# Splitting the experts' block-diagonal fp32 matmuls of an early-fusion network into 64x64 blocks on the four quadrants of TensorE, on one Trainium2 core

## The chip, the cores and the metric

The kernel runs on one core of one Trainium2 chip, in one launch. The metric is device time in microseconds (us) of one execution, the median of several runs. TensorE is called PE here (PEld for its weight loads), VectorE is DVE, ScalarE is ACT, GpSimd is POOL and SyncE is SP.

## What is computed

A small fusion network over 4 batches: a token embedding of `x` (a DFT over patches and a linear layer), concatenation with 77 text tokens, and four residual layers, each behind a layer norm, on a hidden state of 4 batches x 1101 tokens x 64 features. The change is in the second layer, a dense mixture of 8 experts. Cut to what matters:

```python
def _L0_ffn_ref(x, Wr, br, W1, b1, g1, be1, m1, v1, W2, b2, g2, be2, m2, v2, Wo, bo):
    feat = jnp.mean(x, axis=0)
    w = jax.nn.softmax(feat @ Wr + br, axis=-1)
    h = jnp.einsum('bfd,edh->bfeh', x, W1) + b1
    h = jax.nn.relu(_bn(h, g1, be1, m1, v1))
    h = jnp.einsum('bfeh,ehk->bfek', h, W2) + b2
    h = jax.nn.relu(_bn(h, g2, be2, m2, v2))
    y = jnp.einsum('bfeh,ehd->bfed', h, Wo) + bo
    return jnp.einsum('bfed,fe->bfd', y, w)
```

The other layers are an mLSTM (before it), a Mamba block with a selective scan, and a token-selecting MLP (both behind it). All data is fp32.

## The kernel before, in words

**Layout.** Features lie on partitions. Two batches share the 128 partitions: batch 2p on partitions 0 to 63 and batch 2p+1 on 64 to 127, for the pairs p = 0 and 1 (`NPAIR` = 2). The hidden state `H` is [128, 2, 1104], tokens on the free axis (1101 padded to 1104). The tokens go in `NG` = 3 groups of `G` = 368. So that one matmul can do both batches of a pair, the host makes each 64x64 expert weight into a 128x128 block-diagonal one (`diag2` in `pack`); half of such a matrix is zero. PSUM is one tensor `PS` of 8 banks.

**The expert stage** walks n = 0 to 23, which is 3 token groups x 8 experts (k = n // 8, e = n % 8), with one instruction stream on each engine, in program order, tied by semaphores:

- PE, per n, in this order: `layer2(n)` (line 584), `layer1(n+1)` (line 575), `spread_weight(n+1)` (line 592), `layer3(n-1)` (line 600). `layer1`, `layer2` and `layer3` are one 128x128 matmul of 368 columns for each pair p, so two each; an fp32 matmul is two instructions, two passes over the data, in the trace. `layer1` writes banks 2 and 3, `layer2` banks 4 and 5, and `layer3` accumulates over the 8 experts in banks 0 and 1. At the eighth expert `layer3` also adds the experts' output bias by a matmul with `ebias` for each pair (line 605). `spread_weight` is one bf16 matmul that spreads the expert's gate weight over all partitions, into bank 6 or 7.
- ACT, in this order: `hidden2(n)` (line 1023), then `hidden1(n+1)` (line 1015). Each is one activation of 128x736 (both pairs) that reads two PSUM banks and applies the batch norm and the ReLU. Both are recorded by the helper `f`, line 882. The helper serves the whole kernel, so rows of line 882 are told apart by their tiles: those of the experts read `PS,bn_shift,bn_scale`.
- DVE: one multiplication by the spread gate weight (line 1463, 128x736), whose result layer 3 reads; after each eighth expert also the residual addition into `H` (line 1468, 128x736).

**The waits.** `layer2(n)` waits for `hidden1(n)` (its data) and for `hidden2(n-1)` (its banks). `hidden2(n)` waits for `layer2(n)`. `layer1(n+1)` waits for `hidden1(n)` (its banks), `spread_weight(n+1)` and `layer3(n-1)` for the DVE's product of n-1. `layer3` at the first expert of a group waits for the residual addition of the group before. The DVE's product of n waits for `hidden2(n)` and the spread weight.

**Around it.** Ahead of the stage stand the router's logits, its softmax and its transposes (lines 557 to 565). Behind it stand the third layer norm (`ln_pe`, lines 293 and 300; the first of its matmuls waits for all three residual additions, line 622) and `in_proj` of the Mamba block (lines 641 and 646), whose matmuls have 64 rows and 128 columns of weights, two at a time, from partitions 0 to 63 and 64 to 127 into different banks. The longest stage is the selective scan. Its `add_y` (line 735) issues fp32 matmuls with 128 rows and 32 columns of weights, whose outputs go to four different strips of 32 partitions of one bank.

Of the kernel before, what the change touches and what calls it, by code (L numbers as in the profile page):

```python
# [10 lines left out]
ALU = mybir.AluOpType  # L11
# [14 lines left out]
NPAIR = B // 2  # L26
# [4 lines left out]
G = SP // NG  # L31
CG = NC // NG
HC = 64 // L
E = 8
# [42 lines left out]
def build(nc, x, txt, wdft, wts, wexp, bn, out, dbg=None):  # L77
    lay, nw = places(WEIGHTS)
    elay, ne = places(EXPERTS)
    with ExitStack() as ctx:  # L80
# [5 lines left out]
        def s(name):  # L86

            if name not in sems:
                sems[name] = ctx.enter_context(nc.semaphore(name))
            return sems[name]  # L90

        PS = ctx.enter_context(nc.psum_tensor("PS", [128, 8, 512], F32))
        W_ = sb("weights", [128, nw])

        def w(name):
            a, n = lay[name]
            return W_[:, a:a + n]
# [6 lines left out]
        H = sb("hidden", [128, NPAIR, SP])  # L104
        pool_ = sb("pair_arrays", [128, 10, NPAIR, SP])
        P1, P2, P3, P4, P5, P6, P7, P8, P9, P10 = (pool_[:, i] for i in range(10))
# [48 lines left out]
        def ew(name, e):  # L155
            a = elay[name][0] + e * 128
            return EW[:, a:a + 128]

        def twin(a, i):

            return a.rearrange("p a t -> p (a t)")[:, i * NPAIR * G:(i + 1) * NPAIR * G].rearrange("p (a t) -> p a t", a=NPAIR)

        h1b, h2b, hwb = P2, P3, P4
# [7 lines left out]
        wT = P5[:, 0, :]  # L171
# [88 lines left out]
        def cols(k):  # L260
            return slice(k * G, (k + 1) * G)

        def half(b):
            return slice(64 * (b % 2), 64 * (b % 2) + 64)
# [141 lines left out]
        def _(pe):  # L406

            pe.wait_ge(s("w_dft_in"), 16)
            for g in range(NOG):
                last = nc.tensor.matmul(PS[:, 4 + g // 4, (g % 4) * OG * PATCH:(g % 4 + 1) * OG * PATCH],  # L410
                                        wd[:, g * 128:(g + 1) * 128], dft, start=True, stop=True)
# [33 lines left out]
            for i in range(NPAIR):  # L445
                last = nc.tensor.transpose(PS[:, 4, i * TXT:(i + 1) * TXT], txt_sb[:, i * 128:(i + 1) * 128],
                                           w("ident")[0:TXT, 0:TXT])
# [20 lines left out]
            for g, (p, k) in enumerate(groups):  # L468
                pe.wait_ge(s("nq_ready"), p + 1)
                if g >= 2:  # L470
                    pe.wait_ge(s("den_ev"), g - 1)
                nc.tensor.matmul(PS[:, 6 + g % 2, 0:G], w("ones"), ik[:, p, cols(k)],
                                 start=True, stop=True).then_inc(s("den_ps"), 1)

            pe.wait_ge(s("gates_ev"), 3 * NGR)
            for n in range(NL):
                lag, p = n // NPAIR, n % NPAIR
# [4 lines left out]
                for k in range(NG):  # L482
                    last = nc.tensor.matmul(PS[:, NG * p + k, 0:size], w("ones"), prod[n % 4][:, k * size:(k + 1) * size],  # L483
                                            start=True, stop=True)
# [35 lines left out]
            for u in range(NPAIR * NT):  # L520
                n = seq_of(u % NT)[1]
# [22 lines left out]
            for g, (p, k) in enumerate(groups):  # L544
                pe.wait_ge(s("msq_in"), p + 1)
                if g >= 2:
                    pe.wait_ge(s("rms_ev"), g - 1)
                nc.tensor.matmul(PS[:, 6 + g % 2, 0:G], w("ones"), WV[1][:, p, cols(k)],
                                 start=True, stop=True).then_inc(s("msq_ps"), 1)
# [19 lines left out]
            pe.wait_ge(s("ln_ln"), 2 * NGR)  # L569
            NX = NG * E  # L570

            def layer1(n):
                if n >= 1:
                    pe.wait_ge(s("h1_ev"), n)
                for p in range(NPAIR):
                    last = nc.tensor.matmul(PS[:, 2 + p, 0:G], ew("E1", n % E), P1[:, p, cols(n // E)],  # L576
                                            start=True, stop=True)
                last.then_inc(s("l1_ps"), 1)

            def layer2(n):  # L580
                pe.wait_ge(s("h1_ev"), n + 1)
                if n >= 1:
                    pe.wait_ge(s("h2_ev"), n)
                for p in range(NPAIR):
                    last = nc.tensor.matmul(PS[:, 4 + p, 0:G], ew("E2", n % E), twin(h1b, n % 2)[:, p, :],  # L585
                                            start=True, stop=True)
                last.then_inc(s("l2_ps"), 1)

            def spread_weight(n):
                if n >= 2:  # L590
# [4 lines left out]
            def layer3(n):  # L595
                k, e = n // E, n % E
                pe.wait_ge(s("hw_ready"), n + 1)
                if e == 0 and k >= 1:
                    pe.wait_ge(s("ffn_out"), k)
                for p in range(NPAIR):  # L600
                    last = nc.tensor.matmul(PS[:, p, 0:G], ew("E3", e), twin(hwb, n % 2)[:, p, :],  # L601
                                            start=(e == 0), stop=False)
                    if e == E - 1:
                        pe.wait_ge(s("bias_weights"), 1)
                        last = nc.tensor.matmul(PS[:, p, 0:G], w("ebias"), wT[:, cols(k)], start=False, stop=True)
                last.then_inc(s("l3_ps"), 1)

            layer1(0)
# [145 lines left out]
            for g in range(NGR + 2):  # L754
                if g < NGR:
                    p, k = groups[g]
# [519 lines left out]
        def _(dve):  # L1276
# [180 lines left out]
            for n in range(NG * E + 1):  # L1457
                if n < NG * E:
                    dve.wait_ge(s("h2_ev"), n + 1)
                    dve.wait_ge(s("spread_w"), n + 1)  # L1460
                    if n >= 2:
                        dve.wait_ge(s("l3_ps"), n - 1)
                    tt(twin(hwb, n % 2), twin(h2b, n % 2), PS[:, 6 + n % 2:7 + n % 2, 0:G].to_broadcast([128, NPAIR, G]),  # L1463
                       ALU.mult).then_inc(s("hw_ready"), 1)
                if n and n % E == 0:
                    k = n // E - 1
                    dve.wait_ge(s("l3_ps"), n)
                    tt(H[:, :, cols(k)], PS[:, 0:2, 0:G], H[:, :, cols(k)], ALU.add).then_inc(s("ffn_out"), 1)
            dve.wait_ge(s("ffn_out"), NG)
            ln_dve(dve, 3, P1, P3)  # L1470
            dve.wait_ge(s("a_exp"), 1)
# [244 lines left out]
```

## Time and profile before

| | before |
|---|---|
| median of 3 runs | 1158.6 us (1155.54 to 1161.16) |
| the profiled execution | 1158.26 us |
| its span, first to last instruction | 1156.5 us |
| mean granted TensorE clock | 0.74 of full |
| PE busy / weight loads | 873.5 us (76%) / 399.5 us |
| DVE, ACT, POOL busy | 799.4 us (69%), 526.9 us (46%), 553.7 us (48%) |
| expert stage | from 383.9 us to about 486 us |

The profile's times are from the start of the span. A timeline view merges neighbouring instructions of one line into one row: start, time from the first start to the last end, line, operation, tiles, shape, and how many ("x4"); in brackets the idle time ahead of it on its engine and what ended it. The shape "128*64" of a matmul is rows times columns of its weights. Matmuls are pipelined, so a row of four spaced by 0.31 us lasts three spacings and the duration of one.

### The profile page before, as it was taken

How to read it: one execution, taken by the hardware profiler on the slowest of the kernel's cores; microseconds unless marked ns; L12 is line 12 of the kernel's file. 1: busy time of each engine (PE TensorE's matmuls, PEld its weight loads, DVE VectorE, ACT ScalarE, POOL GpSimd, SP SyncE). 2: the span in 40 equal slices, each digit the busy share in tenths (PEclk: the TensorE clock that was granted, in tenths of full speed). 3: DMA queues.
4: the chain of work that ended last, by engine and by line, in shares of the span. 5: the costliest groups of instructions: out<-in, count | busy, mean ns of one | idle time of the engine just before them, and what ended most of it. 6: DMA issues, size and time to landing. Idle time of an engine off the chain costs nothing.

```text
span 1156.5 us, 10951 instructions
## 1 busy us (share of the span) xinstructions
PE 873.5 (76%) x3525; PEld 399.5 (35%) x3525; DVE 799.4 (69%) x1034; ACT 526.9 (46%) x1022; POOL 553.7 (48%) x357
## 2 busy tenths in 40 slices
PE   5587055574966799986578888888878878888787
PEld 3244023463854466553211111111111111114466
DVE  0133889887624222214699999999999999995375
ACT  0237240026544344465755555555555444443631
POOL 0000654950010000000089999999999999982100
PEclk9799578558756899999766677666575575567987
DMA  9900000160100000000110011001101110100001
GB/s 223 175 0 1 0 0 0 31 129 1 37 19 1 1 0 1 1 1 0 40 39 17 24 40 40 21 19 40 41 14 26 40 35 14 31 1 0 1 15 26
DMA packets 28246, 33.05 MB, mean 29 GB/s; under 512 B 10142, under 2 KB 27550, under 8 KB 27678
## 3 DMA queue, kind: packets, MB, share of 16 engines
q1 hardware_dynamic: 28190, 32.36, 12.6%
q8 instruction: 28, 0.46, 0.2%
q14 instruction: 28, 0.23, 0.1%
HBM read 17.57 MB, written 1.20 MB: 16 GB/s over the span
## 4 chain that ended last, share of the span: by engine, by line
PE 39%; DVE 31%; issue 12%; ACT 9%; POOL 4%; SPq 2%; DMA 2%; DVEq 0%; POOLq 0%; ACTq 0%
DVE pair_arrays L1531 12%; DVE pair_arrays L1515 5%; PE PS L735 4%; PE PS L576 3%; PE PS L585 3%; PE PS L707 3%; PE PS L601 2%; ACT pair_arrays L882 2%; PE PS L717 2%; PE PS L512 2%; DMA big<-in_x 2%; PE PS L827 2%; DVE pair_arrays L1367 2%; ACT PS L882 2%; PE PS L483 2%
## 5 line engine op out<-in xcount | busy, mean ns | idle before, releaser
L1225 POOL TENSOR_TENSOR pair_arrays<-pair_arrays 128x736 f32<-128x736 f32 x192 | 332.4, 1745 | 24.0 <-DVE pair_arrays L1531 23.6
L882 ACT ACTIVATE PS<-PS,A_negative 128x368 f32<-128x368 f32 x384 | 191.3, 538 | 131.4 <-PE PS L717 130.9
L1531 DVE TENSOR_TENSOR_SCAN pair_arrays<-PS,scan_carry,pair_arrays 128x368 f32<-128x368 f32 x256 | 236.2, 964 | 0.4
L735 PE MATMUL PS<-pair_arrays,weights 128*32 128x368 f32 x768 | 134.5, 731 | 1.1 <-POOL pair_arrays L1225 1.0
L1515 DVE TENSOR_TENSOR pair_arrays<-pair_arrays,PS 128x736 f32<-128x736 f32 x144 | 129.0, 896 | 7.1 <-PE PS L707 7.0
L1187 POOL TENSOR_TENSOR big<-pair_arrays 128x1104 f32<-128x1104 f32 (+15 forms) x32 | 60.5, 1908 | 152.9 <-DVE pair_arrays L1321 117.1
L1531 DVE TENSOR_TENSOR_SCAN pair_arrays<-PS,pair_arrays 128x368 f32<-128x368 f32 x128 | 110.3, 904 | 2.2 <-ACT PS L882 2.2
L707 PE MATMUL PS<-spread_rows,token_weights 96*128 96x368 bf16 x192 | 70.9, 466 | 38.6 <-DVE pair_arrays L1515 25.1
L1233 POOL TENSOR_TENSOR pair_arrays<-pair_arrays,token_weights 128x736 f32<-128x736 f32 x48 | 84.0, 1750 | 29.7 <-DVE big L1501 29.7
L1246 POOL TENSOR_TENSOR pair_arrays<-big 128x368 f32<-128x368 f32 x24 | 18.7, 799 | 161.6 <-DVE big L1501 161.6
L707 PE MATMUL PS<-pair_arrays,token_weights 96*128 96x368 bf16 x192 | 64.3, 427 | 28.1 <-DVE pair_arrays L1515 21.7
L483 PE MATMUL PS<-big,weights 128*128 128x368 f32 (+15 forms) x192 | 57.4, 463 | 34.3 <-DVE big L1378 23.6
L717 PE MATMUL PS<-spread_rows,token_weights 96*128 96x368 bf16 x192 | 72.7, 476 | 7.2 <-DVE pair_arrays L1531 5.4
L717 PE MATMUL PS<-pair_arrays,token_weights 96*128 96x368 bf16 x192 | 65.2, 432 | 17.0 <-DVE pair_arrays L1531 15.7
L882 ACT ACTIVATE pair_arrays<-pair_arrays 128x69 f32<-128x69 f32 (+4 forms) x43 | 27.2, 636 | 109.0 <-DVE pair_arrays L1367 72.6
L882 ACT ACTIVATE pair_arrays<-PS,bn_shift,bn_scale 128x736 f32<-128x736 f32 x48 | 46.3, 964 | 57.4 <-PE PS L585 42.3
L1463 DVE TENSOR_TENSOR pair_arrays<-pair_arrays,PS 128x736 f32<-128x736 f32 x24 | 22.1, 921 | 71.0 <-ACT pair_arrays L882 71.0
L882 ACT ACTIVATE pair_arrays<-PS,weights 128x368 f32<-128x368 f32 (+1 forms) x66 | 38.3, 594 | 49.2 <-PE PS L827 33.0
L483 PEld LDWEIGHTS PS<-big,weights 128*128 128x128 f32 x192 | 42.6, 271 | 49.4 <-issue 32.3
L882 ACT ACTIVATE pair_arrays<-PS 64x256 f32<-64x256 f32 (+5 forms) x54 | 26.2, 499 | 72.9 <-PE PS L512 18.2
L882 ACT ACTIVATE scan_carry<-pair_arrays 128x2 f32<-128x2 f32 x128 | 26.3, 206 | 69.6 <-DVE pair_arrays L1531 69.2
L882 ACT ACTIVATE token_weights<-PS 128x736 f32<-128x736 f32 (+2 forms) x66 | 44.2, 670 | 25.1 <-PE PS L707 19.9
(192 smaller groups left out, 1393.2 us busy)
## 6 DMA issues: line engine op xcount, KB each, us to landing
big<-in_x SPq DMA_DIRECT2D x8, 1024.0 KB, 21.4
big<-decay_rows SPq DMA_DIRECT2D x4, 1104.0 KB, 14.7
spread_rows<-pair_arrays SPq DMA_DIRECT2D x96, 46.0 KB, 2.0
pair_arrays<-pair_arrays SPq DMA_DIRECT2D x96, 46.0 KB, 1.9
spread_rows<-big SPq DMA_DIRECT2D x48, 46.0 KB, 1.9
pair_arrays<-big SPq DMA_DIRECT2D x48, 46.0 KB, 1.9
weights<-in_wts SPq DMA_DIRECT2D x1, 2204.0 KB, 21.3
big<-in_wexp SPq DMA_DIRECT2D x1, 1536.0 KB, 7.5
```

What stands on the lines that cost most here:

```text
L483: last = nc.tensor.matmul(PS[:, NG * p + k, 0:size], w("ones"), prod[n % 4][:, k * size:(k + 1) * size], start=True, stop=True)
L576: last = nc.tensor.matmul(PS[:, 2 + p, 0:G], ew("E1", n % E), P1[:, p, cols(n // E)], start=True, stop=True)
L585: last = nc.tensor.matmul(PS[:, 4 + p, 0:G], ew("E2", n % E), twin(h1b, n % 2)[:, p, :], start=True, stop=True)
L707: last = nc.tensor.matmul(PS[:, 2 + h, 0:G], pick[:, (i // 2) * 128:(i // 2 + 1) * 128], high(stack[seg % 2][1][0:3 * DB, 2 * (i % 2) + h] ...
L717: last = nc.tensor.matmul(PS[:, 4 + 2 * (t % 2) + h, 0:G], pick[:, (i // 2) * 128:(i // 2 + 1) * 128], high(stack[seg % 2][0][0:3 * DB, 2 ...
L735: last = nc.tensor.matmul(PS[r:r + DB, seg % 2, 0:G], w("ysel")[:, (i // 2) * DB:(i // 2 + 1) * DB], hcbuf[t % NRING][:, h, :], start=Fals ...
L882: return nc.scalar.activation(o, i, fn, **kw)
L1187: nc.gpsimd.tensor_tensor(prod[n % 4][:, 0:NC * (L - lag)].rearrange("p (c r) -> p c r", r=L - lag), chunks(q_[:, p, :])[:, :, lag:L], chu ...
L1225: nc.gpsimd.tensor_tensor(hcbuf[t % NRING], hbuf[t % NRING], c4(seg).unsqueeze(1).to_broadcast([128, 2, G]), ALU.mult).then_inc(s("hc_read ...
L1233: nc.gpsimd.tensor_tensor(bx[t % NRING], b4(t // NSTEP).unsqueeze(1).to_broadcast([128, 2, G]), moved, ALU.mult).then_inc(s("bx_ready"), 1)
L1515: tt(bx[t % NRING], b4(seg).unsqueeze(1).to_broadcast([128, 2, G]), PS[:, 2:4, 0:G], ALU.mult).then_inc(s("b_used"), 1)
L1531: nc.vector.tensor_tensor_scan(hbuf[t % NRING][:, h, :], PS[:, 4 + 2 * (t % 2) + h, 0:G], bx[t % NRING][:, h, :], carry[:, a:a + 1] if k e ...
```

## The change

The two pairs' matmuls of each expert layer are issued as four 64x64 blocks in place of two 128x128 block-diagonal matrices: batch half b2 of pair p reads weight rows and data of its own 64 partitions and writes 64 PSUM partitions. For p = 0 the output lands on the half of its input, for p = 1 on the other half, so that the four blocks take the four (row half, column half) positions of the array. The data of pair 1 is thus swapped after layer 1, back after layer 2, and swapped again after layer 3, where the residual addition undoes it. The bank of a pair is as before, and the semaphore is counted up by the last matmul as before. The bias matmuls stay 128x128 and now both follow the four blocks. The ACT instructions, the gate product and `spread_weight` are unchanged. The host's weights are unchanged; the blocks are cut from the diagonal.

```diff
+            def both_pairs(bank, weight, data, start, stop):
+
+                for p in range(NPAIR):
+                    for b2 in range(2):
+                        last = nc.tensor.matmul(PS[half((b2 + p) % 2), bank + p, 0:G], weight[half(b2), 64 * b2:64 * b2 + 64],
+                                                data[half(b2), p, :], start=start, stop=stop, skip_group_check=True)
+                return last
+
             def layer1(n):
                 if n >= 1:
                     pe.wait_ge(s("h1_ev"), n)
-                for p in range(NPAIR):
-                    last = nc.tensor.matmul(PS[:, 2 + p, 0:G], ew("E1", n % E), P1[:, p, cols(n // E)],
-                                            start=True, stop=True)
-                last.then_inc(s("l1_ps"), 1)
+                both_pairs(2, ew("E1", n % E), P1[:, :, cols(n // E)], True, True).then_inc(s("l1_ps"), 1)
 
             def layer2(n):
                 pe.wait_ge(s("h1_ev"), n + 1)
                 if n >= 1:
                     pe.wait_ge(s("h2_ev"), n)
-                for p in range(NPAIR):
-                    last = nc.tensor.matmul(PS[:, 4 + p, 0:G], ew("E2", n % E), twin(h1b, n % 2)[:, p, :],
-                                            start=True, stop=True)
-                last.then_inc(s("l2_ps"), 1)
+                both_pairs(4, ew("E2", n % E), twin(h1b, n % 2), True, True).then_inc(s("l2_ps"), 1)
...
                 pe.wait_ge(s("hw_ready"), n + 1)
                 if e == 0 and k >= 1:
                     pe.wait_ge(s("ffn_out"), k)
-                for p in range(NPAIR):
-                    last = nc.tensor.matmul(PS[:, p, 0:G], ew("E3", e), twin(hwb, n % 2)[:, p, :],
-                                            start=(e == 0), stop=False)
-                    if e == E - 1:
-                        pe.wait_ge(s("bias_weights"), 1)
-                        last = nc.tensor.matmul(PS[:, p, 0:G], w("ebias"), wT[:, cols(k)], start=False, stop=True)
+                last = both_pairs(0, ew("E3", e), twin(hwb, n % 2), e == 0, False)
+                if e == E - 1:
+                    pe.wait_ge(s("bias_weights"), 1)
+                    for p in range(NPAIR):
+                        last = nc.tensor.matmul(PS[:, p, 0:G], w("ebias"), wT[:, cols(k)], start=False, stop=True,
+                                                skip_group_check=True)
                 last.then_inc(s("l3_ps"), 1)
...
                 if n and n % E == 0:
                     k = n // E - 1
                     dve.wait_ge(s("l3_ps"), n)
-                    tt(H[:, :, cols(k)], PS[:, 0:2, 0:G], H[:, :, cols(k)], ALU.add).then_inc(s("ffn_out"), 1)
+                    tt(H[:, 0, cols(k)], PS[:, 0, 0:G], H[:, 0, cols(k)], ALU.add)
+                    for b2 in range(2):
+                        ins = tt(H[half(b2), 1, cols(k)], PS[half(1 - b2), 1, 0:G], H[half(b2), 1, cols(k)], ALU.add)
+                    ins.then_inc(s("ffn_out"), 1)
```

## Rows read from the trace of the kernel before

**Rows 1.** The page's second part: 40 slices of the span, in tenths.
```profile
PE   5587055574966799986578888888878878888787
PEclk9799578558756899999766677666575575567987
```

**Rows 2.** Busy time of each engine in chosen stretches, granted clock, DMA share, GB/s.
```profile
389.38:480.70 91.32, 90.42 (x304) 54.36 (x303) 23.03 (x25) 44.33 (x46) 0.00 (x0) 1.00 0.00 1
```

**Rows 3.** Timeline of one expert step, all engines.
```profile
430.44 0.96 ACT L882 ACTIVATE pair_arrays<-PS,bn_shift,bn_scale 128x736 f32<-128x736 f32 x1 [0.27 <-PE PS L576]
431.63 1.40 PE L585 MATMUL PS<-pair_arrays,big 128*128 128x368 f32 x4
432.87 1.40 PE L576 MATMUL PS<-pair_arrays,big 128*128 128x368 f32 x4
433.07 0.96 ACT L882 ACTIVATE pair_arrays<-PS,bn_shift,bn_scale 128x736 f32<-128x736 f32 x1 [1.67 <-PE PS L585]
434.07 0.92 DVE L1463 TENSOR_TENSOR pair_arrays<-pair_arrays,PS 128x736 f32<-128x736 f32 x1 [2.94 <-ACT pair_arrays L882]
434.11 0.32 PE L592 MATMUL PS<-pair_arrays,big 128*128 128x368 bf16 x1
434.26 1.40 PE L601 MATMUL PS<-pair_arrays,big 128*128 128x368 f32 x4
434.31 0.96 ACT L882 ACTIVATE pair_arrays<-PS,bn_shift,bn_scale 128x736 f32<-128x736 f32 x1 [0.27 <-PE PS L576]
```

**Rows 4.** Timeline of the stage's first instructions.
```profile
383.91 2.79 PE L576 MATMUL PS<-pair_arrays,big 128*128 128x368 f32 x4 [1.67 <-issue]
386.82 0.96 ACT L882 ACTIVATE pair_arrays<-PS,bn_shift,bn_scale 128x736 f32<-128x736 f32 x1 [8.79 <-PE PS L576]
387.84 1.50 PE L585 MATMUL PS<-pair_arrays,big 128*128 128x368 f32 x4 [0.91 <-ACT pair_arrays L882]
389.38 0.96 ACT L882 ACTIVATE pair_arrays<-PS,bn_shift,bn_scale 128x736 f32<-128x736 f32 x1 [1.60 <-PE PS L585]
```

**Rows 5.** Timeline of the selective scan, line 735, three windows.
```profile
593.51 0.52 PE L735 MATMUL PS<-pair_arrays,weights 128*32 128x368 f32 x4
593.51 0.82 PE L735 MATMUL PS<-pair_arrays,weights 128*32 128x368 f32 x8
602.81 1.46 PE L735 MATMUL PS<-pair_arrays,weights 128*32 128x368 f32 x8
```

**Rows 6.** Timeline of the Mamba input projection, line 641, two windows.
```profile
504.20 0.49 PE L641 MATMUL PS<-pair_arrays,token_weights 64*128 64x368 f32 x2
504.20 0.80 PE L641 MATMUL PS<-pair_arrays,token_weights 64*128 64x368 f32 x4
```

**Rows 7.** Timeline of the scan where line 735 follows a 128x128 matmul.
```profile
701.68 0.78 PE L724 MATMUL PS<-big,D_diagonal 128*128 128x368 f32 x2
702.40 0.81 PE L735 MATMUL PS<-pair_arrays,weights 128*32 128x368 f32 x4
```

**Rows 8.** Timeline of ACT in the input projection: two activations back to back.
```profile
503.80 0.87 ACT L882 ACTIVATE big<-PS,weights 128x736 f32<-128x736 f32 x1 [1.82 <-PE PS L641]
504.57 0.78 ACT L882 ACTIVATE big<-PS 128x736 f32<-128x736 f32 x1
```

**Rows 9.** Timeline of the stage's end.
```profile
480.70 0.96 ACT L882 ACTIVATE pair_arrays<-PS,bn_shift,bn_scale 128x736 f32<-128x736 f32 x1 [1.67 <-PE PS L585]
482.67 0.89 PE L601 MATMUL PS<-pair_arrays,big 128*128 128x368 f32 x2 [0.77 <-DVE pair_arrays L1463]
484.63 0.78 PE L605 MATMUL PS<-pair_arrays,weights 128*128 128x368 f32 x2
485.45 0.93 DVE L1468 TENSOR_TENSOR hidden<-PS,hidden 128x736 f32<-128x736 f32 x1 [2.83 <-PE PS L605]
```

**Rows 10.** Groups of instructions: a DVE addition from PSUM of 128x368.
```profile
L1537 DVE TENSOR_TENSOR big<-big,PS 128x368 f32<-128x368 f32 x12 | 6.1, 511 | 3.4 <-PE PS L735 3.4
```

**Rows 11.** Busy time in further stretches: clock, and PE's densest issuing (PE, PEld counts).
```profile
189.00:199.00 10.00, 4.67 (x18) 3.03 (x18) 9.83 (x9) 0.74 (x3) 6.89 (x4) 1.00 0.00 0
199.00:205.70 6.70, 5.50 (x12) 3.69 (x12) 6.60 (x6) 0.57 (x2) 3.16 (x2) 0.50 0.00 0
940.00:953.00 13.00, 8.56 (x44) 2.09 (x48) 12.77 (x16) 5.87 (x12) 13.00 (x8) 1.00 0.30 71
965.00:1017.00 52.00, 46.32 (x169) 10.27 (x168) 51.19 (x61) 25.33 (x50) 48.83 (x31) 0.50 0.09 22
1147.80:1152.50 4.70, 4.70 (x49) 4.70 (x49) 3.09 (x11) 0.00 (x0) 0.00 (x0) 1.00 0.22 45
309.00:313.00 4.00, 3.85 (x35) 3.72 (x34) 4.00 (x1) 1.01 (x4) 0.00 (x0) 0.50 0.00 0
```

## The prediction

> **What bounds the kernel now.** Start with the 40 slices: PE is busy for 7 to 9 tenths in slices 15 and 16 and the granted clock is at its full value there [rows 1]. The busy times of the stretch from the first `hidden2` to the last (389.38 to 480.70 us) make it sharp: 91.32 us, PE busy for 90.42 of them at clock 1.00, that is at 2.4 GHz, ACT for 44.33, DVE for 23.03 [rows 2]. So the expert stage, 8% of the span, is bound by PE, and no other engine is half full. The timeline of one step shows how [rows 3]. A step takes 434.31 - 430.44 = 3.87 us. In it PE issues three layers of four passes (two pairs, two passes for fp32), each 1.24 us after the one before (431.63, 432.87), and one bf16 matmul 0.15 us ahead of the next layer: 3 x 1.24 + 0.15 = 3.87. One pass therefore takes (1.40 - 0.47) / 3 = 0.31 us, 0.47 us being the duration of a single one (in a row of two, 0.78 - 0.31 [rows 7]). ACT waits 1.67 us for layer 2 and 0.27 us for layer 1.
>
> **What the change does to PE's work.** Each layer becomes four blocks of two passes. If the four blocks run at once, a layer costs 2 x 0.31 = 0.62 us in place of 1.24. No row shows blocks split in rows and columns together, so I bound it from both sides. Split by columns: in line 735 four passes start together and last 0.52 us, and all eight of four strips are over in 0.82 us at full clock [rows 5], where eight in sequence would need 7 x 0.31 + 0.47 = 2.64. Split by rows: in line 641 two start together and last 0.49 us, four are over in 0.80 [rows 6]. Both kinds of tile overlap completely, and they do so first passes first, not held up by the second pass of the first tile. At worst the two kinds don't combine and only two run at once: 1.24 us a layer, as now. I take four at once, because both neighbours behave so, and keep the other as a rival.
>
> The first pass behind an idle PE is longer by the weight load. With 128 columns two passes take 0.89 us, so the second starts after 0.89 - 0.47 = 0.42 [rows 9]; with 32 columns after 0.82 - 0.47 - 0.02 = 0.33 [rows 5]. For 64 columns I interpolate 0.36 us.
>
> **Two changes of array shape a step** are added, into and out of `spread_weight`. Line 724 is 128x128: its second pass starts at 701.68 + 0.31 = 701.99 and has streamed by 702.30; the 32-column tiles start at 702.40 [rows 7]. A change costs 0.10 us. PE's step is then 0.67 (layer 2) + 0.62 (layer 1) + 0.10 + 0.15 + 0.10 + 0.62 (layer 3) = 2.3 us.
>
> **The new bound** is the ring between ACT and layer 2. `hidden1(n+1)` ends; layer 2 starts 0.06 later (387.84 against 386.82 + 0.96 [rows 4]); 0.36 to its second pass, 0.47 for that, 0.02 of skew between tiles (0.80 against 0.31 + 0.47 [rows 6]), 0.04 until `hidden2` starts (389.38 against 387.84 + 1.50 [rows 4]): 0.95 us in place of 1.67. `hidden2` and `hidden1(n+1)` then follow each other, because, counted from layer 2's first pass, layer 1 and its semaphore are through after 0.67 + 0.62 + 0.20 = 1.5 us and `hidden2` ends only after 0.89 + 0.96 = 1.85. Two such activations back to back start 0.77 us apart where the first lasts 0.87 [rows 8], so 0.10 overlaps: 0.86 + 0.96. The ring is 0.95 + 0.86 + 0.96 = 2.77 us, longer than PE's 2.3, so the shape changes and layer 3 lie beside it. DVE's product (0.92 us [rows 3]) starts when `hidden2` ends and is done before `spread_weight` two steps on asks for it.
>
> **The sum.** From the first `hidden2` to the last: now 91.32. After: 23 x 2.77 = 63.7, plus two group boundaries. At a boundary the four bias passes (1.24 now as then) and one more shape change make PE's step 2.3 + 0.10 + 1.24 + 0.10 = 3.74, that is 0.97 over the ring, twice. 65.6 us: 25.7 saved. The residual addition inside the stage becomes three instructions; one of 128x368 from PSUM took 0.511 us [rows 10], halves of partitions no less, so 3 x 0.51 less two overlaps of 0.05 = 1.43 in place of 0.93 [rows 9]. At the first two boundaries it ends about 5.4 us after that step's start, and layer 3 of the next step asks for it at 3.74 + 1.65 = 5.4: just covered. If the cover fails, each costs some 0.3.
>
> Start: layer 1 of n = 0 runs at 1.2 GHz and takes 2.91 us until ACT starts [rows 4]; eight passes of four tiles took 1.46 at that clock [rows 5], so 1.5: 1.4 saved. But PE is then idle more of the time before 386.8, where the clock rose, and may rise later. A step at 1.2 GHz is PE-bound: 6 x 0.62 + 0.31 + 0.2 = 4.2 us, 1.4 over. So 0 to 1.4; I take 0.7. End: from layer 3's start to the last bias pass 2.74 us now (482.67 to 485.41 [rows 9]); then 0.36 + 0.31 + 0.10 + 1.40 = 2.17: 0.57 saved, and 0.50 given back by the last addition, which the layer norm waits for: 0.1.
>
> 25.7 + 0.7 + 0.1 = 26.5 us. The profiled execution took 1158.26, 0.3 below the median of 1158.6: 1158.3 - 26.5 = 1131.8, predicted as 1132. **The forecast's own range:** without overlap on ACT and with 0.42 for the first pass the ring is 2.98, 4.8 us more; uncovered additions 0.6; later stages move against the free changes of clock, and the runs of before differ by 5.6 among themselves. So 1127 to 1140. About 0.5% (5.8 us) is what a measurement of this kernel can tell from no change.
>
> **Rivals.** *PE's issuing becomes the bound.* A step has 25 weight loads and 25 passes in place of 13 and 13, and five waits: 55 entries. The densest stretches issued 98 in 4.70 us, 48 ns each, and 69 in 4.00, 58 ns (64-column weights) [rows 11]. That is 2.6 to 3.2 us a step against a ring of 2.77. At the upper end 0.4 x 23 = 9 more: 1141. For it: the range straddles the ring. Against it: PE fetches ahead while it waits. Chance 0.11.
>
> *The clock falls.* PE would be busy for about 2.45 of 2.77 us as these views count (last pass to its end), 0.88. Stretches at full clock that ended in a fall had 0.47 (189 to 199) and 0.66 (940 to 953), while at 1.2 GHz PE stayed down with 0.89 (965 to 1017) [rows 11]. 0.88 is well above what fell, yet a fall would not be undone quickly. In full it costs 4.2 a step, PE-bound: 1132 + 23 x 1.4 = 1164. Half the stage at either level is likelier: 1148. Chance 0.07.
>
> *The blocks overlap only in pairs*, no more than line 641's, so that the change doesn't do what it says: 3.87 + 2 x 0.10 = 4.07 a step, 4.6 over all, 0.5 for the last addition: 1163. Nothing in the rows is for it except that no four with different rows are seen. Chance 0.04.
>
> *The slower one: blocks with different rows in one bank take turns.* Line 641's pairs write different banks; here the two blocks of a pair write the two halves of one bank, and they are issued next to each other. If the second waits for the first and the queue keeps its order, the passes fall into slots: T1 | T2 and T3 | T4 and T1 again, and so on. Four slots a layer, and one more for each of the two runs of a step (shape changes cut it where spread_weight stands): 13 to 14 slots of 0.31 + 0.15 + 0.20 = 4.5 us. That is 0.6 over 3.87, 24 times, less the overlaps at the boundaries: 1158 + 12 = 1170. It decides as soon as a layer takes over four slots. Chance 0.10.
> The Trainium skill speaks for this rival: "TensorEngine Tiling (Array Packing)", section "Gotcha 1: PSUM Pressure", says that different row tiles cannot access the same PSUM bank simultaneously. By that rule the time would be near 1170 and not 1132; no row here shows such a pair. Its section "Key Properties" says that a change of tiling mode drains TensorE; by that rule each step has two drains, and the 0.10 us of rows 7 agrees with a small one.
>
> **Chances.** Forecast 0.68, issuing 0.11, clock 0.07, pairs only 0.04, turns 0.10. Faster by over 0.5%: 0.68 + 0.11 + 0.06 = 0.85. Within 0.5%: 0.04 and a little of the clock's case, 0.05. Slower: 0.10. The range 1127 to 1150 takes in the forecast, the issuing case and most of the clock's, and leaves out the last two.
>
> **What would show it.** Right: ACT's instructions of the stage start alternately 0.86 and about 1.9 us apart, `hidden2` waits 0.95 us on layer 2 and `hidden1` waits on nothing; passes of both_pairs in fours, 0.02 us apart; clock 1.00 from 390 us to the end of the stage; the stage some 26 us shorter and PE busy for less of it; three additions in place of each residual one. Wrong: `hidden2` still idle for 1.6 us or more (pairs or turns); ACT idle ahead of `hidden1`, with PE waiting on nothing (issuing); clock 0.50 in the stage. The time itself over 1150 would refute the forecast.

## The result and the profile after

| | before | after |
|---|---|---|
| median | 1157.1 us (4 runs, 1155.54 to 1161.16) | 1131.79 us (4 runs, 1130.93 to 1136.78) |
| ratio, 95% interval | | 0.9763 [0.9728, 0.9797] |
| profiled execution, span | 1158.26, 1156.5 us | 1131.17, 1129.4 us |
| first `hidden2` to the last | 91.32 us | 66.70 us |
| one step of the expert stage | 3.87 us | 2.79 us |

The change is faster by 2.4%. The forecast was 1132 us, and the two profiled spans differ by 27.1 us where 26.5 were forecast. The medians differ by 25.3 us, and the interval of the ratio allows 23.5 to 31.5. So that the median lies within 0.3 us of the forecast is luck; what tests the forecast is the length of a step and of the stage.

The page's second part for the changed kernel, against [rows 1]:

```profile
PE   5587045576776699796588877878878878878887
PEclk9799568568756599898667688565585575567987
```

The busy times of three stretches of its expert stage (PE, PEld, DVE, ACT, POOL, clock, DMA share, GB/s), against [rows 2]:

```profile
385.76:390.30 4.54, 3.43 (x18) 0.90 (x17) 0.90 (x1) 2.65 (x3) 0.00 (x0) 0.50 0.00 0
388.35:455.05 66.70, 60.54 (x579) 20.04 (x575) 24.42 (x29) 41.95 (x46) 0.00 (x0) 0.99 0.01 1
390.40:455.00 64.60, 58.91 (x570) 19.93 (x574) 23.50 (x28) 40.16 (x45) 0.00 (x0) 1.00 0.01 1
```

The clock is at its lower level until about 390.3 us and full from there to the end of the stage. PE still shows 91% busy (58.91 of 64.60), a number that misleads: it counts each pass to its end, so PE looks busy although it could start the next passes earlier (a step that PE bounds takes 2.28 us and not 2.79, see e4). The timeline of one step is clearer, against [rows 3]. `both_pairs` is a helper, so all three layers have its line, 576, and `x16` is layer 2 followed at once by layer 1; ACT's rows have line 884 now:

```profile
422.36 1.47 PE L576 MATMUL PS<-pair_arrays,big 64*64 64x368 f32 x16 [0.28 <-ACT pair_arrays L884]
423.28 1.82 ACT L884 ACTIVATE pair_arrays<-PS,bn_shift,bn_scale 128x736 f32<-128x736 f32 x2 [0.97 <-PE PS L576]
423.76 0.33 PE L594 MATMUL PS<-pair_arrays,big 128*128 128x368 bf16 x1
424.02 0.85 PE L576 MATMUL PS<-pair_arrays,big 64*64 64x368 f32 x8
424.28 0.92 DVE L1465 TENSOR_TENSOR pair_arrays<-pair_arrays,PS 128x736 f32<-128x736 f32 x1 [1.87 <-ACT pair_arrays L884]
425.15 1.47 PE L576 MATMUL PS<-pair_arrays,big 64*64 64x368 f32 x16 [0.28 <-ACT pair_arrays L884]
```

Sixteen passes last 1.47 us, which is three spacings of 0.31, a first one of some 0.05 more, and one tail. ACT's two evictions are one row of 1.82 us (0.86 + 0.96), and ACT waits 0.97 us for layer 2 and for nothing else. PE, which hardly stood still before, now waits 0.28 us for ACT in each step.

A timeline with a narrow window shows single groups of passes. Four start together (the first row behind a change of shape, the second the last four of layer 1), and the bf16 matmul follows 0.42 us behind the latter (a slot of 0.31 and the change of shape, 0.11):

```profile
392.25 0.54 PE L576 MATMUL PS<-pair_arrays,big 64*64 64x368 f32 x4
408.31 0.49 PE L576 MATMUL PS<-pair_arrays,big 64*64 64x368 f32 x4
408.73 0.33 PE L594 MATMUL PS<-pair_arrays,big 128*128 128x368 bf16 x1
```

At the group boundaries and at the end of the stage, against [rows 9]:

```profile
412.56 1.50 PE L606 MATMUL PS<-pair_arrays,weights 128*128 128x368 f32 x4
414.10 0.54 DVE L1470 TENSOR_TENSOR hidden<-PS,hidden 128x368 f32<-128x368 f32 x1 [1.15 <-PE PS L606]
414.66 1.09 DVE L1472 TENSOR_TENSOR hidden<-PS,hidden 64x368 f32<-64x368 f32 x2
414.91 1.82 ACT L884 ACTIVATE pair_arrays<-PS,bn_shift,bn_scale 128x736 f32<-128x736 f32 x2 [2.06 <-PE PS L576]
415.89 1.43 PE L576 MATMUL PS<-pair_arrays,big 64*64 64x368 f32 x12 [0.17 <-DVE hidden L1472]
...
434.44 1.82 ACT L884 ACTIVATE pair_arrays<-PS,bn_shift,bn_scale 128x736 f32<-128x736 f32 x2 [0.97 <-PE PS L576]
438.31 1.82 ACT L884 ACTIVATE pair_arrays<-PS,bn_shift,bn_scale 128x736 f32<-128x736 f32 x2 [2.06 <-PE PS L576]
...
457.02 0.85 PE L576 MATMUL PS<-pair_arrays,big 64*64 64x368 f32 x8 [1.42 <-DVE pair_arrays L1465]
457.80 1.50 PE L606 MATMUL PS<-pair_arrays,weights 128*128 128x368 f32 x4
459.35 0.54 DVE L1470 TENSOR_TENSOR hidden<-PS,hidden 128x368 f32<-128x368 f32 x1 [2.38 <-PE PS L606]
461.14 1.48 PE L293 MATMUL PS<-hidden,weights 128*128 128x368 f32 x4 [1.83 <-DVE hidden L1472]
```

The step with the bias takes 438.31 - 434.44 = 3.87 us, 1.08 over the others, at both boundaries.

**Where the 27.1 us come from.** The stage is entered 0.20 us later (384.11 against 383.91). From there to the first `hidden2` 1.24 us are saved (388.35 against 389.38). From the first to the last `hidden2` 24.62 are saved (91.32 - 66.70). From the last to the layer norm's first matmul 0.27 are lost (461.14 - 455.05 = 6.09 against 486.52 - 480.70 = 5.82). Behind that the kernel is 1.7 us shorter, 1.3 of it in the selective scan, which the change does not touch.

### The profile page after: what moved, and what is told of

Same layout as the page of the kernel before. It is cut to its first block, busy times and chain, and to the rows that moved or that the text cites. A ratio compares the mean times of both kernels' runs of the same rounds, so it can differ in the third digit from the quotient of the medians.

```text
span 1129.4 us, 11533 instructions
## 1 busy us (share of the span) xinstructions
PE 840.9 (74%) x3813; PEld 362.9 (32%) x3813; DVE 801.2 (71%) x1040; ACT 524.3 (46%) x1022; POOL 553.6 (49%) x357
## 4 chain that ended last, share of the span: by engine, by line
PE 34%; DVE 32%; issue 14%; ACT 11%; POOL 4%; SPq 2%; DMA 2%; DVEq 0%; ACTq 0%; POOLq 0%
DVE pair_arrays L1536 13%; DVE pair_arrays L1520 5%; ACT pair_arrays L884 4%; PE PS L737 3%; PE PS L576 3%; PE PS L709 2%; PE PS L719 2%; PE PS L512 2%; DMA big<-in_x 2%; ACT PS L884 2%; PE PS L829 2%; POOL pair_arrays L1227 2%; DVE pair_arrays L1369 2%; PE PS L483 2%; SPq L360 2%
## 5 line engine op out<-in xcount | busy, mean ns | idle before, releaser
L1520 DVE TENSOR_TENSOR pair_arrays<-pair_arrays,PS 128x736 f32<-128x736 f32 x144 | 129.0, 896 | 5.7 <-PE PS L709 5.5
L576 PE MATMUL PS<-pair_arrays,big 64*64 64x368 f32 x576 | 57.5, 501 | 10.0 <-ACT pair_arrays L884 6.5
L884 ACT ACTIVATE pair_arrays<-PS,bn_shift,bn_scale 128x736 f32<-128x736 f32 x48 | 43.9, 960 | 33.9 <-PE PS L576 33.9
```

The costliest lines, as they stand in the source:

```text
L576: last = nc.tensor.matmul(PS[half((b2 + p) % 2), bank + p, 0:G], weight[half(b2), 64 * b2:64 * b2 + 64], data[half(b2), p, :], start=start ...
L884: return nc.scalar.activation(o, i, fn, **kw)
L1520: tt(bx[t % NRING], b4(seg).unsqueeze(1).to_broadcast([128, 2, G]), PS[:, 2:4, 0:G], ALU.mult).then_inc(s("b_used"), 1)
```

## The experiments

All ratios are against the kernel before, run on the same chip; steps are from the start of one of ACT's evictions to the same one of the next step, in the profile. Each edit is against the changed kernel unless it says otherwise. None leaves work out.

**e1, two positions of the array.**

```diff
-                        last = nc.tensor.matmul(PS[half((b2 + p) % 2), bank + p, 0:G], weight[half(b2), 64 * b2:64 * b2 + 64],
+                        last = nc.tensor.matmul(PS[half(b2), bank + p, 0:G], weight[half(b2), 64 * b2:64 * b2 + 64],
...
-                    tt(H[:, 0, cols(k)], PS[:, 0, 0:G], H[:, 0, cols(k)], ALU.add)
-                    for b2 in range(2):
-                        ins = tt(H[half(b2), 1, cols(k)], PS[half(1 - b2), 1, 0:G], H[half(b2), 1, cols(k)], ALU.add)
-                    ins.then_inc(s("ffn_out"), 1)
+                    tt(H[:, :, cols(k)], PS[:, 0:2, 0:G], H[:, :, cols(k)], ALU.add).then_inc(s("ffn_out"), 1)
```

> The changed kernel, but pair 1 is not swapped: all blocks sit on two positions of the array, (rows 0-63, columns 0-63) and (rows 64-127, columns 64-127), and the residual addition is one instruction again. Theory A (the gain is four blocks at once, each position for itself): only two blocks run together, a layer is four slots of 0.31 us as before the change, a step 3.87 + 0.2 for the two shape changes, about 4.07, and the time about 1157 + 4 = 1161. Theory B (the gain comes from smaller matrices as such: half the weight load and no zero rows): a step stays near 2.8 and the time near 1131. Theory C (blocks with different rows that write one bank take turns): eight slots a layer, 2.5 us, a step above 7 us, over 1230.

Measured: 1165.64 us, ratio 1.004 [1.002, 1.006], a step of 4.12 us. The timeline of ACT and PE, and a window of 0.1 us at 413.5 (the row of x4):

```profile
413.12 0.79 PE L576 MATMUL PS<-pair_arrays,big 64*64 64x368 f32 x4
...
414.57 0.96 ACT L884 ACTIVATE pair_arrays<-PS,bn_shift,bn_scale 128x736 f32<-128x736 f32 x1 [0.27 <-PE PS L576]
414.72 3.93 PE L576 MATMUL PS<-pair_arrays,big 64*64 64x368 f32 x24
417.46 0.96 ACT L884 ACTIVATE pair_arrays<-PS,bn_shift,bn_scale 128x736 f32<-128x736 f32 x1 [1.92 <-PE PS L576]
```

Four passes now last 0.79 us, two after two, where the changed kernel's last 0.49 to 0.54. 24 passes take 3.93 us against 2.32 (1.47 + 0.85). So the form 64x64 by itself gives nothing, and costs 0.25 us a step over the kernel before: two shape changes of 0.10, and 0.05 by which the first pass behind a change is longer. The whole gain needs all four positions. And the two blocks of this kernel have different rows and write the two halves of one bank. They start together, so nothing takes turns there.

**e2 and e3, more work on PE.** Both kernels with `spread_weight` issued three times:

```diff
-                nc.tensor.matmul(PS[:, 6 + n % 2, 0:G], pick8[:, (n % E) * 128:(n % E + 1) * 128], wTb[:, cols(n // E)],
-                                 start=True, stop=True).then_inc(s("spread_w"), 1)
+                for _ in range(3):
+                    last = nc.tensor.matmul(PS[:, 6 + n % 2, 0:G], pick8[:, (n % E) * 128:(n % E + 1) * 128], wTb[:, cols(n // E)],
+                                            start=True, stop=True)
+                last.then_inc(s("spread_w"), 1)
```

> The changed kernel with spread_weight's matmul issued three times into the same bank: 0.31 us more PE work in each of 24 steps. Theory A (the ring of ACT's two evictions and layer 2 binds, PE has 0.4 us of slack): unchanged, within 1.5 us of the changed kernel, 1131. Theory B (PE's queue with its shape changes or its issuing still binds): + 7 us, 1138.

> The kernel before with the same two extra issues of spread_weight's matmul in each step. Both theories have PE as the bound there: + 0.31 x 23 = 7 us, 1164. If it does not slow down, the measure of slack in the other run is worth nothing.

Measured: the changed kernel with it 1131.25 us, ratio 0.9734 [0.9709, 0.976], its step still 2.79. The kernel before with it 1165.06 us, ratio 1.0037 [1.002, 1.0055]; its step went from 3.87 to 4.18, the 0.31 to the hundredth. From its first `hidden1` to its last `hidden2` it is 7.2 us longer (101.06 against 93.88), as forecast, but the medians differ by 4.1 only; why the later stages gave some back was not looked into. ACT's timeline in e2, then in e3 (with the rows of `spread_weight`):

```profile
429.50 1.82 ACT L886 ACTIVATE pair_arrays<-PS,bn_shift,bn_scale 128x736 f32<-128x736 f32 x2 [0.97 <-PE PS L576]
429.98 0.64 PE L595 MATMUL PS<-pair_arrays,big 128*128 128x368 bf16 x3
432.29 1.82 ACT L886 ACTIVATE pair_arrays<-PS,bn_shift,bn_scale 128x736 f32<-128x736 f32 x2 [0.97 <-PE PS L576]
```

```profile
431.79 0.96 ACT L884 ACTIVATE pair_arrays<-PS,bn_shift,bn_scale 128x736 f32<-128x736 f32 x1 [1.98 <-PE PS L585]
432.82 0.63 PE L593 MATMUL PS<-pair_arrays,big 128*128 128x368 bf16 x3
435.96 0.96 ACT L884 ACTIVATE pair_arrays<-PS,bn_shift,bn_scale 128x736 f32<-128x736 f32 x1 [1.97 <-PE PS L585]
```

In a plain step the same extra work is paid in full before the change and not at all after it. PE's queue no longer sets the step; of PE's work only layer 2 is still on the critical path, as a part of the ring. The two steps with the bias are different: in e2 they take 4.19 us where the changed kernel's take 3.87, so there PE still binds and the 0.31 is paid.

**e8 and e9, one part of the change alone.** e8 puts layer 2 back to 128x128 (and the residual addition to one instruction, because pair 1 is back in place); e9 keeps only layer 2 in blocks, with layers 1 and 3 as they were before the change. The diff is that of layer 2 in e8.

```diff
-                both_pairs(4, ew("E2", n % E), twin(h1b, n % 2), True, True).then_inc(s("l2_ps"), 1)
+                for p in range(NPAIR):
+                    last = nc.tensor.matmul(PS[:, 4 + p, 0:G], ew("E2", n % E), twin(h1b, n % 2)[:, p, :], start=True, stop=True)
+                last.then_inc(s("l2_ps"), 1)
```

> The changed kernel with layer 2 as 128x128 matmuls again (layers 1 and 3 stay in blocks, so pair 1 is swapped back by layer 3 and the residual addition is one instruction). Theory A (ring): layer 2 in isolation is 0.06 + 0.42 + 2 x 0.31 + 0.47 + 0.04 = 1.61, the ring 1.61 + 0.86 + 0.96 = 3.43 us a step, above PE's 0.62 + 0.62 + 1.24 + 0.15 + four shape changes of 0.1 = 3.03; the time about 15 us over the changed kernel, 1146. Theory B (PE's sum alone decides): 3.03 us a step, 6 us over, 1137.

> Only layer 2 in blocks, layers 1 and 3 as 128x128 matmuls. Here the ring (2.79) is shorter than PE's 1.24 + 0.67 + 1.24 + 0.15 + two shape changes of 0.1 = 3.5 us: theory A and theory B both say 3.5 us a step, about 8 us under the kernel before, 1150. A step of 2.8 would mean that only layer 2's length counts.

Measured: e8 1149.86 us, ratio 0.9913 [0.9885, 0.9942], a step of 3.42 us. e9 1152.88 us, 0.993 [0.9907, 0.9953], a step of 3.61. ACT's timeline, e8 and then e9:

```profile
413.39 1.82 ACT L887 ACTIVATE pair_arrays<-PS,bn_shift,bn_scale 128x736 f32<-128x736 f32 x2 [1.59 <-PE PS L590]
416.80 1.82 ACT L887 ACTIVATE pair_arrays<-PS,bn_shift,bn_scale 128x736 f32<-128x736 f32 x2 [1.59 <-PE PS L590]
```

```profile
412.80 0.96 ACT L889 ACTIVATE pair_arrays<-PS,bn_shift,bn_scale 128x736 f32<-128x736 f32 x1 [1.24 <-PE PS L576]
414.21 0.96 ACT L889 ACTIVATE pair_arrays<-PS,bn_shift,bn_scale 128x736 f32<-128x736 f32 x1 [0.44 <-PE PS L584]
416.41 0.96 ACT L889 ACTIVATE pair_arrays<-PS,bn_shift,bn_scale 128x736 f32<-128x736 f32 x1 [1.24 <-PE PS L576]
```

e8 tells the theories apart: 3.42 is the ring with the long layer 2 (3.43 forecast), not PE's sum of 3.03. In e9 ACT waits for both layers and PE's sum decides. It came out 0.1 over the 3.5 forecast: I had left out the first pass of layer 1 behind a shape change, 0.42 in place of 0.31. Of the step of 3.87 us, e8 saves 0.45 and e9 0.26; all three layers in blocks save 1.08. The first is held by the ring, the second by PE.

**e4 and e5, the ring taken off the path.** The two streams reordered so that layer 2 runs while ACT evicts layer 1 of the next step; e5 is the same on the kernel before.

```diff
             layer1(0)
             spread_weight(0)
+            layer1(1)
             for n in range(NX):
                 layer2(n)
-                if n + 1 < NX:
-                    layer1(n + 1)
-                    spread_weight(n + 1)
-                if n >= 1:
-                    layer3(n - 1)
+                if n >= 2:
+                    layer3(n - 2)
+                if n + 2 < NX:
+                    layer1(n + 2)
+                if n + 1 < NX:
+                    spread_weight(n + 1)
+            layer3(NX - 2)
             layer3(NX - 1)
...
             for n in range(NG * E):
-                hidden2(n)
                 if n + 1 < NG * E:
                     hidden1(n + 1)
+                hidden2(n)
```

> The changed kernel with ACT's order turned to hidden1(n+1), hidden2(n), and PE's to layer2(n), layer3(n-2), layer1(n+2), spread_weight(n+1), so that layer 2 runs while ACT does hidden1. Theory A: the ring falls to two evictions of 0.9 us and PE's 2.3 us binds: 0.45 us less in each of some 22 steps, 10 us less than the changed kernel, 1121. Theory B (PE binds already): unchanged, 1131.

> The kernel before with the same reordering of ACT and PE as in e4. Theory A (before the change PE's passes bind, the ring of evictions and layer 2 only after it): steps stay at 3.87 us, the time within 3 us of the kernel before. Theory B (the reordering helps by itself, whatever the matmuls' form): 10 us less, as in e4.

Measured: e4 1122.43 us, ratio 0.9661 [0.963, 0.9692], a step of 2.28 us. e5 1155.84 us, 0.9964 [0.9947, 0.9981], its step 3.87 as before; its small gain (3.6 us between the medians, 2.3 in the stage of the trace: 91.56 us from the first `hidden1` to the last `hidden2` where the kernel before has 93.88) lies in its first steps. ACT in e4, then in e5:

```profile
415.02 2.02 ACT L887 ACTIVATE pair_arrays<-PS,bn_shift,bn_scale 128x736 f32<-128x736 f32 x2 [0.50 <-PE PS L576]
417.31 2.00 ACT L887 ACTIVATE pair_arrays<-PS,bn_shift,bn_scale 128x736 f32<-128x736 f32 x2 [0.27 <-PE PS L576]
```

```profile
414.06 0.96 ACT L885 ACTIVATE pair_arrays<-PS,bn_shift,bn_scale 128x736 f32<-128x736 f32 x1 [1.51 <-PE PS L576]
417.92 0.96 ACT L885 ACTIVATE pair_arrays<-PS,bn_shift,bn_scale 128x736 f32<-128x736 f32 x1 [1.51 <-PE PS L576]
```

A reordering worth 0.51 us a step after the change gives a step nothing before it, which shows that the ring binds only since the change. 2.28 is also the measure of PE's own step, forecast as 2.3.

**e6 and e7, no shape changes.** `spread_weight` in two 64x64 blocks, in e6 on the changed kernel and in e7 on e4:

```diff
+                for h in range(2):
+                    last = nc.tensor.matmul(PS[half(h), 6 + n % 2, 0:G], pick8[0:64, (n % E) * 128 + 64 * h:(n % E) * 128 + 64 * h + 64],
+                                            wTb[0:64, cols(n // E)], start=True, stop=True, skip_group_check=True)
```

> e4 with spread_weight split into two 64x64 blocks (rows 0-63 only, which hold all the gates; both column halves), so that a step has no change of array shape. Theory A (e4's step of 2.28 us is PE's passes plus two shape changes of 0.1 us): a step of 2.1 us, 4 us less than e4, 1118. If the shape changes cost nothing on a PE-bound step: 2.28 us and e4's time, 1122.

> The changed kernel (ACT's order as it was) with spread_weight in two 64x64 blocks, so that no step changes the array's shape. Theory A (the ring of 2.79 us binds, the shape changes lie in PE's slack): a step of 2.79 us and the changed kernel's time, ratio to the kernel before 0.976. Theory B (shape changes cost the changed kernel 0.2 us a step): 2.6 us a step, 4.5 us less, ratio 0.972.

Measured: e6 1132.63 us, ratio 0.9765 [0.9748, 0.9782], a step of 2.79 or 2.80: nothing, as theory A has it. Only its two steps with the bias are shorter, 3.60 us where the changed kernel's take 3.87. e7 1120.82 us, 0.966 [0.9623, 0.9696], steps of 2.01 and 2.09 in turn, but as a whole no better than e4 beyond the noise, where 4 us were forecast. ACT's timeline in e7:

```profile
420.08 1.82 ACT L889 ACTIVATE pair_arrays<-PS,bn_shift,bn_scale 128x736 f32<-128x736 f32 x2 [0.27 <-PE PS L576]
422.10 1.82 ACT L889 ACTIVATE pair_arrays<-PS,bn_shift,bn_scale 128x736 f32<-128x736 f32 x2 [0.20 <-PE PS L576]
424.19 1.82 ACT L889 ACTIVATE pair_arrays<-PS,bn_shift,bn_scale 128x736 f32<-128x736 f32 x2 [0.27 <-PE PS L576]
```

So e4 and e7 ran once more, side by side:

> e4 once more, beside the next run on one chip: steps of 2.28 us, ratio 0.966. It is the base for the next run, whose 4 us in the stage did not show in the whole time when the two ran in different calls.

> e7 once more, beside e4. If the 4.2 us that its expert stage is shorter reach the end: ratio 0.0036 below e4's, 0.9625. If later stages give them back (their clock falls at other places): the ratio of e4, 0.966, and the later stages longer by 4 us in the trace.

Measured: e4b 1123.5 us, 0.9671 [0.9646, 0.9697]; e7b 1120.28 us, 0.9658 [0.9645, 0.9671]. The intervals overlap; the stage up to the Mamba block is 5.6 us shorter in e7b (74.80 against 80.40), the medians differ by 3.2. The busy times of the stage and of the selective scan, e7b, then e4b:

```profile
385.50:460.30 74.80, 65.78 (x654) 32.31 (x652) 30.90 (x41) 53.83 (x67) 0.00 (x0) 0.96 0.01 1
550.00:1011.30 461.30, 381.19 (x1538) 84.25 (x1537) 448.37 (x529) 240.71 (x545) 438.11 (x280) 0.64 0.11 28
```

```profile
386.70:467.10 80.40, 72.19 (x630) 28.95 (x629) 30.94 (x41) 56.07 (x67) 0.00 (x0) 0.94 0.00 1
555.70:1013.70 458.00, 368.41 (x1538) 81.77 (x1537) 447.99 (x529) 240.58 (x545) 437.79 (x280) 0.69 0.11 28
```

3.3 us are given back in the scan, whose work is the same (x1538 passes in both) at a mean clock of 0.64 in place of 0.69. (e7's own scan had taken 458.1 us at 0.69.) The kernel before has 461.3 us at 0.64 too. Why the scan takes the one course or the other was not tried; the shift of its start is the likely cause, argued only.

**e10, the bias in blocks too**, on e7:

```diff
-                    for p in range(NPAIR):
-                        last = nc.tensor.matmul(PS[:, p, 0:G], w("ebias"), wT[:, cols(k)], start=False, stop=True,
-                                                skip_group_check=True)
+                    last = both_pairs(0, w("ebias"), wT[:, cols(k)].unsqueeze(1).to_broadcast([128, NPAIR, G]), False, True)
...
+            pool.wait_ge(s("win_ready"), 1)
+            step(nc.gpsimd.tensor_copy(wT[64:96], wTb[0:32]))
...
-        "ebias": rows(np.tile(f["L0_ffn_bo"], (3, 2))),
+        "ebias": twice(rows(np.tile(f["L0_ffn_bo"], (3, 2)))[0:64]),
```

> e7 with the bias matmuls as four blocks too (the gates are also laid on partitions 64 to 95, by one more GpSimd copy, and the bias rows on rows 64 to 87 of the weights): 0.62 us in place of 1.24 and two shape changes of 0.1, three times, 2.5 us less than e7 in the stage, ratio 0.002 below e7's.

Measured: 1115.17 us, ratio 0.9615 [0.9595, 0.9635], the fastest of all. The forecast of 2.5 us holds: the two steps around each group boundary take 5.33 us together where e7's take 6.14, and from the last `hidden2` to the layer norm it is 5.30 us where e7 has 6.08, so each of the three biases saves 0.8, 2.4 in all. Of its lead of 5.1 us over e7b, 3.2 lie in the scan, which took 458.1 us at clock 0.69, the scan's other course. The four blocks of a bias, eight passes, in its timeline:

```profile
408.19 0.83 PE L576 MATMUL PS<-pair_arrays,weights 64*64 64x368 f32 x8
```

## Why the prediction was right

**Four blocks at once.** Right, and the step on which all rested. Four passes last 0.49 us where one lasts 0.47, and e1 shows that two positions alone gain nothing (ratio 1.004). The bound from two separate kinds of tile [rows 5, 6] carried over to their combination.

**The ring.** Right to 0.02 us: 2.79 against 2.77, made of a wait of 0.97 (0.95 forecast) and 1.82 for the two evictions, as forecast. e2 and e3 show that PE's queue no longer binds a plain step, e8 that layer 2's length enters the ring, e4 and e5 that the order of the evictions and layers is what closes it. One sum on it was wrong: the upper end of the ring, without overlap and with 0.42 for the first pass, was given as 2.98, but these two terms make it 2.77 + 0.10 + 0.06 = 2.93. The range would have been about 1 us narrower.

**PE's step of 2.3 us and the shape changes of 0.10.** Right: e4 is bound by it at 2.28, and e7 without the two changes has a mean of 2.05, so 0.11 each, in which the 0.05 us for the longer first pass is included. (The Trainium skill, "TensorEngine Tiling (Array Packing)", "Key Properties", says that a change of mode drains TensorE; these numbers agree and price it.) In a plain step of the changed kernel they cost nothing (e6); in its two steps with the bias, which PE bounds, e6 saves 0.27.

**The sum.** 26.5 forecast; 25.6 in and around the stage (24.62 + 1.24 - 0.27), and 1.7 behind it, which the forecast had only in its range. That the sum came out within 0.6 us of 27.1 owes something to these 1.7, which is luck: the stage itself gave 0.9 less than forecast. Of its terms, three were mis-sized, each by less than a microsecond. *The steps*: 25.7 forecast; 24.62, or 25.0 without the one step that the late clock stretched to 3.16 us, which I had put into the start. The ring is 0.02 longer in 23 steps, and a boundary costs 1.08 over it and not 0.97. What was missing there are the first passes behind a change of shape, which also wait for their weights: the first bias pass 0.42 in place of 0.31, the first of layer 3 0.36. Layer 3 of the next group did wait 0.17 us (at 415.89) for the residual addition that I had called just covered, but that cost nothing: `hidden2` had started at 414.91, and the next step took 2.79 again. *The start*: 0.7 forecast as 1.4 less half a slow step; it measured 1.24 - 0.37 = 0.87. *The end*: 0.1 forecast, 0.27 lost. The additions took 0.54 + 1.09 and a gap of 0.01, 1.64 us in place of 1.43, because each took 0.54 and not 0.51, and they don't overlap as I had assumed; layer 3 and the bias took 2.28 (457.02 to 459.30) in place of 2.17, because the first bias pass behind the change of shape also waits for its weights. (One reading of the prediction is loose, and nothing hangs on it: slices 15 and 16 of [rows 1] both read 9 for PE, not 7 to 9.)

**The rivals.** *Turns of blocks in one bank* (the slower one) is refuted. In e1 the two blocks of each bank start together, and in the changed kernel all four do. The Trainium skill's rule, "TensorEngine Tiling (Array Packing)", "Gotcha 1: PSUM Pressure", that different row tiles cannot access the same bank simultaneously, is not borne out for blocks that write different halves of the partitions; the measurement decides. Whether it holds for the same partitions was not tried. *Pairs only* is what e1 is, at 1.004, and the real kernel is not it. *Issuing*: e7 issues 26 loads and 26 passes in 2.05 us, 39 ns each on average, so the 48 to 58 ns I had read from [rows 11] were no limit of issuing. *The clock*: 1.00 from 390.4 to 455.0. Its rise was late by one step only. In e6, whose plain steps are as long, it came later still (granted clock 0.50 to 390 us, 0.57 on average from there to 396), and ACT's timeline shows three long steps:

```profile
385.35 0.97 ACT L886 ACTIVATE pair_arrays<-PS,bn_shift,bn_scale 128x736 f32<-128x736 f32 x1 [7.52 <-PE PS L576]
...
389.17 0.97 ACT L886 ACTIVATE pair_arrays<-PS,bn_shift,bn_scale 128x736 f32<-128x736 f32 x1 [0.26 <-PE PS L576]
...
392.99 0.97 ACT L886 ACTIVATE pair_arrays<-PS,bn_shift,bn_scale 128x736 f32<-128x736 f32 x1 [0.26 <-PE PS L576]
395.57 1.82 ACT L886 ACTIVATE pair_arrays<-PS,bn_shift,bn_scale 128x736 f32<-128x736 f32 x2 [1.62 <-PE PS L576]
398.37 1.82 ACT L886 ACTIVATE pair_arrays<-PS,bn_shift,bn_scale 128x736 f32<-128x736 f32 x2 [0.97 <-PE PS L576]
```

The first two are 3.82 us from `hidden1` to `hidden1`; ACT waits 1.62 and 0.26 us in them. So a late rise costs about 1 us in each of the first two steps. The 4.2 us that I had worked out for PE at the lower level were not tested: these two steps have no layer 3 in PE's queue yet, the third (3.44 us) saw the clock rise, and no trace shows a whole later step at the lower level.

## What to carry to other kernels

A block-diagonal matrix that joins two small contractions wastes half the array. Splitting it paid here only with the blocks of both pairs on four different (rows, columns) positions; on two positions it was a slight loss. When the bound engine is made twice as fast, write down the ring of waits that comes next: here it kept 0.5 us of each step from PE, and a reordering that shortened the stage by 2.3 us before the change shortened it by 10.0 us after it (e5 and e4, first `hidden1` to last `hidden2`). Judge such edits by the length of their own stage, since a later stage can move by 3 us through its clock alone.

## What the hardware showed that I had not expected

- Two blocks with different rows that write different halves of one PSUM bank run at once: four fp32 passes of 64x64x368 last 0.49 us where one lasts 0.47.
- A VectorE addition on 64 partitions (538 ns mean, below) takes as long as one on 128 (541 ns), so splitting the residual addition by halves costs a full instruction. The groups of instructions of DVE in the changed kernel's stage:

```profile
L1472 DVE TENSOR_TENSOR hidden<-PS,hidden 64x368 f32<-64x368 f32 x6 | 3.2, 538 | 0.1
L1470 DVE TENSOR_TENSOR hidden<-PS,hidden 128x368 f32<-128x368 f32 x3 | 1.6, 541 | 4.7 <-PE PS L606 4.7
```

- The selective scan, the same instructions in each kernel, took 458 us at a mean clock of 0.69 or 460 to 461 us at 0.64, with nothing changed in it.
